# Four convolution layers on one core: the last part of the dense sum on two engines, its statistics partly combined early, the first pair's taps apart, and the loads for the next image in another order

## What is computed

```
# _gn: groups of 2 channels, mean and variance over the group's pixels
x = x + depthwise(_gn(x), kernels from means, w1, b1, w2, b2)   # layer 0
x = x + conv3x3(sign(_gn(x)), sign(W))                          # layer 1, dense over 32 channels
x = x + depthwise(_gn(x), ...)                                  # layer 2
x = x + depthwise(_gn(x), ...)                                  # layer 3
# depthwise: pooled = mean of each channel; hdn = relu(pooled @ w1 + b1);
# kernels = hdn @ w2 + b2, one 3x3 filter for each image and channel
```

## Times and the profile before

| | us |
|---|---|
| median of three runs | 4344.64 |
| lowest and highest | 4337.99, 4358.8 |
| the profiled execution, device time | 4354.15 |
| its span in the trace | 4352.3 |
| TensorE busy | 3142.5 (72% of the span) |
| VectorE, ScalarE, POOL busy | 2069.2, 1786.4, 1957.0 |

### The profile page before, as it was taken

One profiled execution on the slowest core, in us unless ns is written; L12 is line 12 of the kernel. 1 busy time (PEld: TensorE's weight loads), 2 busy tenths in 40 slices (PEclk: granted clock), 3 DMA queues, 4 the chain that ended last, 5 costly groups with the idle time before them and its releaser, 6 DMA issues.

```text
span 4352.3 us, 69714 instructions
## 1 busy us (share of the span) xinstructions
PE 3142.5 (72%) x26176; PEld 2008.6 (46%) x26176; DVE 2069.2 (48%) x6038; ACT 1786.4 (41%) x2626; POOL 1957.0 (45%) x3175
## 2 busy tenths in 40 slices
PE   0675987758876588865887667867778759777598
PEld 0443645435454354633545434554445535445355
DVE  2626643266432764327543275333844257432573
ACT  2433633335333463434534354333543436324232
POOL 1326544264432653336533464425643265431754
PEclk9987998879988798987998879888889889888799
DMA  6288697876969769596694967969678697786946
GB/s 210 57 147 168 151 318 200 155 164 140 340 175 170 159 159 322 159 195 153 182 330 119 212 148 197 306 118 216 149 217 292 109 212 165 234 270 111 200 76 218
DMA packets 589270, 829.46 MB, mean 191 GB/s; under 512 B 489731, under 2 KB 490502, under 8 KB 572550
## 3 DMA queue, kind: packets, MB, share of 16 engines
q1 hardware_dynamic: 323200, 734.28, 66.5%
q10 hardware_dynamic: 216582, 76.68, 8.2%
q0 software_dynamic: 49152, 14.05, 2.0%
HBM read 375.89 MB, written 267.45 MB: 148 GB/s over the span
## 4 chain that ended last, share of the span: by engine, by line
PE 46%; DMA 21%; DVE 9%; SPq 8%; ACT 5%; POOL 4%; ACTq 3%; issue 3%; DVEq 0%; POOLq 0%
PE acc L961 26%; PE acc L978 14%; SPq L327 6%; DMA dense_out<-arena 5%; DMA out<-y 4%; DMA arena<-x 4%; POOL y L510 4%; PE acc L1040 3%; DMA arena<-signs 3%; DVE dense_stats L860 2%; DMA signs<-arena 2%; DMA arena<-y 2%; ACT arena L599 2%; ACTq L535 2%; ACTq L606 2%
## 5 line engine op out<-in xcount | busy, mean ns | idle before, releaser
L961 PE MATMUL acc<-y,arena 64*128 64x384 f32 x9216 | 1749.3, 508 | 190.1 <-ACT y L568 129.0
L961 PEld LDWEIGHTS acc<-y,arena 64*128 64x128 f32 x9216 | 1013.6, 197 | 777.4 <-ACT y L568 229.2
L327 POOL DMA_DIRECT2D arena<-y x1536 | 790.6, 522 | 837.3 <-PE acc L978 736.4
L568 ACT ACTIVATE y<-acc 128x768 f32<-128x768 f32 x832 | 645.1, 807 | 1177.5 <-PE acc L978 1176.6
L978 PE MATMUL acc<-arena 64*128 64x384 f32 x4608 | 953.9, 509 | 195.2 <-issue 195.2
L489 POOL TENSOR_SCALAR arena<-arena,cst,fill 128x24 f32<-128x24 f32 (+1 forms) x1536 | 614.3, 419 | 701.8 <-issue 450.4
L510 POOL TENSOR_TENSOR y<-arena,y 128x3072 f32<-128x3072 f16 x88 | 529.8, 6043 | 734.5 <-DMA arena<-dense_out 734.3
L860 DVE BATCH_NORM_STATS2 dense_stats<-y 128x6 f32<-128x192 f32 x1536 | 408.0, 345 | 728.4 <-POOL y L510 728.2
L978 PEld LDWEIGHTS acc<-arena 64*128 64x128 f32 x4608 | 518.1, 196 | 422.3 <-issue 228.2
L1040 PE MATMUL acc<-arena,wd_side 128*32 128x384 fp8e4 (+1 forms) x10752 | 470.4, 329 | 290.3 <-DMA arena<-signs 231.5
L802 DVE TENSOR_SCALAR_CACHE_REDUCE y<-acc 128x768 f32<-128x768 f32 x256 | 245.1, 958 | 624.3 <-PE acc L978 624.3
(11 more groups left out here) (84 smaller groups left out, 1145.6 us busy)
## 6 DMA issues: line engine op xcount, KB each, us to landing
y<-x SPq DMA_DIRECT2D x64, 2304.0 KB, 26.1
out<-y SPq DMA_DIRECT2D x64, 2304.0 KB, 23.6
arena<-y SPq DMA_DIRECT2D x768, 141.0 KB
arena<-x SPq DMA_DIRECT2D x168, 576.0 KB, 6.4
dense_out<-arena ACTq DMA_DIRECT2D x384, 192.0 KB, 6.9
arena<-dense_out SPq DMA_DIRECT2D x192, 384.0 KB, 6.8
arena<-y SPq DMA_DIRECT2D x768, 71.9 KB
arena<-signs SPq DMA_DIRECT2D x192, 250.0 KB, 10.4
```

The costliest lines, as they stand in the source:

```text
L327: eng.dma_start(halo[at:at + n, slot, :, d0:d0 + size], y[source:source + (n - 1) * step + 1:step, first + odd:first + odd + 3:2, s0:s0 + ...
L568: nc.scalar.activation(y[:, 2 * g:2 * g + 2, k * KN:(k + 1) * KN], acc[:, 2 * k:2 * k + 2, 0:KN], ACT.Identity, accum_out=sums[:, g, k:k + ...
L961: nc.tensor.matmul(acc[:, 2 * k + odd, 0:KN], w_center[at, slot, 2 * q + odd, :], y[at, 2 * g + odd, k * KN:(k + 1) * KN], start=turn == 0 ...
```

## The change

There are four parts.

1. End of the dense layer. POOL also adds the upper 8 channels of the twelfth half, VectorE only the lower 8 (`D_SHARED`). The statistics of the first five windows are combined into one block ahead of the last addition; at the end three blocks per channel are combined, of unequal size.
2. Start of each depthwise layer. A small product of 18 columns (`ps_first`) gives the taps of the first pair, ahead of the full product of 288. `first_weights` turns pair 0's centre taps and writes its weights, then batch 0's halo weights, then pair 1's centre, then the rest; what was one pass over all halo taps is now two, and the centre taps take three passes where they took two.
3. Places in the accumulator memory. Means and variances of `li` 1 and `li` 2 go to banks 5 and 4, other small tiles change places between banks 6 and 7, and TensorE's wait for `fill_ready` ahead of the group variance falls away in `li` 1 and `li` 2.
4. Loads for the next image. ScalarE takes statistics g - 1 behind the copies of pair g, where it took statistics g; the last, 23, now falls in `li` 2 behind pair 8. In SP's queue loads 0 and 1 move ahead of the second and third halo batch of `li` 1, and the loads from 3 on move behind a later halo batch. POOL clears the staging area one batch later.

```diff
@@ sync
-                for b in range(HALO_SLOTS):
-                    halos(first + b)
+                halos(first)
                 for i in range(AHEAD_SLOTS):
                     load_ahead(s, i)
+                for b in range(1, HALO_SLOTS):
+                    halos(first + b)
                 for b in range(BATCHES):
-                    load_ahead(s, 2 * b + AHEAD_SLOTS)
                     halos(first + b + HALO_SLOTS)
-                    load_ahead(s, 2 * b + AHEAD_SLOTS + 1)
+                    for i in (2 * b + AHEAD_SLOTS - 1, 2 * b + AHEAD_SLOTS):
+                        if i >= AHEAD_SLOTS:
+                            load_ahead(s, i)
...
-                    for i in range(2):
-                        load_ahead(s, PAIRS + AHEAD_SLOTS + 2 * b + i)
+                    for i in (PAIRS + 1 + 2 * b, PAIRS + 2 + 2 * b):
+                        load_ahead(s, i)
@@ gpsimd
-                        for n in range(WINDOWS * D_HALVES - 1):
+                        for n in range(WINDOWS * D_HALVES):
...
+                            first = D_SHARED if n == WINDOWS * D_HALVES - 1 else 0
...
-                        if li == 2 and s < B - 1 and b == AHEAD_LATE // 2 + 1:
+                        if li == 2 and s < B - 1 and b == AHEAD_LATE // 2 + 2:
                             clean_stage(s + 1)
@@ scalar
                     evict(d + 1, g)
-                    if s < B - 1:
-                        ahead_stats(s, g)
+                    if s < B - 1 and g > 0:
+                        ahead_stats(s, g - 1)
...
-                        if g < AHEAD_LATE:
-                            ahead_stats(s, PAIRS + g)
+                        if g <= AHEAD_LATE:
+                            ahead_stats(s, PAIRS + g - 1)
@@ vector
-            def first_centers(d):
-                dve.wait_ge(taps_ready, d + 1)
-                turn_centers(slice(0, BATCH_CH))
-                center_weights(d, 0, BATCH_PAIRS)
+            def first_weights(d):
+
+                dve.wait_ge(first_taps_ready, d + 1)
+                turn_centers(slice(0, 2), ps_first.rearrange("p (c t) -> p c t", t=TAPS))
+                pair_centers(d, 0)
+                dve.wait_ge(taps_ready, d + 1)
+                turn_halos(slice(0, BATCH_PAIRS))
                 halo_weights(0)
-                turn_centers(slice(BATCH_CH, C))
+                turn_centers(slice(2, BATCH_CH), by_tap[:, 2:BATCH_CH])
+                pair_centers(d, 1)
+                turn_centers(slice(BATCH_CH, C), by_tap[:, BATCH_CH:C])
+                turn_halos(slice(BATCH_PAIRS, PAIRS))
...
@@ vector, dense
+                add_blocks((agg[:, :, 0], agg[:, :, 1]), early, [WN // 2] * (2 * (WINDOWS - 1)))
...
-                at = y[:, D_CH:C, w * WN:(w + 1) * WN]
-                nc.vector.tensor_tensor(at, d_in[:, n % D_SLOTS], at, ALU.add).then_inc(d_added_last, 1)
+                at = y[:, D_CH:D_CH + D_SHARED, w * WN:(w + 1) * WN]
+                nc.vector.tensor_tensor(at, d_in[:, n % D_SLOTS, 0:D_SHARED], at, ALU.add).then_inc(d_added_last, 1)
...
+                add_blocks((agg[:, :, 0], agg[:, :, 1]), end, [(WINDOWS - 1) * WN, WN // 2, WN // 2])
@@ tensor
-                pe.wait_ge(fill_ready, d + 1)
-                group_sums(ps_var, spread[:]).then_inc(group_var_ready, 1)
+                if d % ND == 0:
+                    pe.wait_ge(fill_ready, d + 1)
+                group_sums(ps_var[d % ND], spread[:]).then_inc(group_var_ready, 1)
...
+                nc.tensor.matmul(ps_first, hidden[:], w2_sb[:, li, 0:2 * TAPS], start=False, stop=True)\
+                    .then_inc(first_taps_ready, 1)
                 nc.tensor.matmul(ps_taps, hidden[:], w2_sb[:, li, :], start=False, stop=True).then_inc(taps_ready, 1)
```

More of the change, by code:

```diff
@@ L70 @@
 D_CH = C // D_HALVES
+D_SHARED = D_CH // 2
 A_HALO = 0
@@ L861, in window_stats, with add_blocks @@
                 return last
+            def add_blocks(to, blocks, counts):
+                means, spreads = blocks[:, :, :, 1], blocks[:, :, :, 2]
+                n = means.shape[2]
+                whole = sum(counts)
+                mean, spread_of = to
+                if len(set(counts)) == 1:
+                    link(nc.vector.tensor_reduce(mean, means, AX.X, ALU.add))
+                    link(nc.vector.tensor_scalar(mean, mean, 1.0 / n, None, ALU.mult))
+                    link(nc.vector.tensor_tensor(means, means, mean.unsqueeze(2).to_broadcast([P, C, n]), ALU.subtract))
+                    link(nc.vector.scalar_tensor_tensor(means, means, float(counts[0]), means, ALU.mult, ALU.mult))
+                else:
+                    weights = dense_stats[:, :, 0, 0:n]
+                    part = dense_stats[:, :, 1, 0:n]
+                    link(nc.vector.tensor_tensor(part, means, weights, ALU.mult))
+                    link(nc.vector.tensor_reduce(mean, part, AX.X, ALU.add))
+                    link(nc.vector.tensor_scalar(mean, mean, 1.0 / whole, None, ALU.mult))
+                    link(nc.vector.tensor_tensor(means, means, mean.unsqueeze(2).to_broadcast([P, C, n]), ALU.subtract))
+                    link(nc.vector.tensor_tensor(part, means, weights, ALU.mult))
+                    link(nc.vector.tensor_tensor(means, means, part, ALU.mult))
+                link(nc.vector.tensor_tensor(spreads, spreads, means, ALU.add))
+                link(nc.vector.tensor_reduce(spread_of, spreads, AX.X, ALU.add))
             def dense(s):
-                adds = WINDOWS * D_HALVES - 1
+                adds = WINDOWS * D_HALVES
                 for w in range(WINDOWS - 1):
@@ L867, in dense @@
                         dve.wait_ge(d_added, s * adds + w * D_HALVES + half + 1)
-                        window_stats(w, half)
+                        last = window_stats(w, half)
+                link(last)
+                rows = dense_stats[:].rearrange("p c w s -> p c (w s)")
+                early = rows[:, :, 0:6 * (WINDOWS - 1)].rearrange("p c (b k) -> p c b k", k=3)
+                end = rows[:, :, 6 * (WINDOWS - 1) - 3:].rearrange("p c (b k) -> p c b k", k=3)
+                add_blocks((agg[:, :, 0], agg[:, :, 1]), early, [WN // 2] * (2 * (WINDOWS - 1)))
```

127 lines of the change are left out of this document (66 added, 61 removed).

## The result

The changed kernel takes 4552.57 us (median of 4, 4547.59 to 4558.82), the kernel before 4345.62 (median of 4): a ratio of 1.0461, with a 95% interval of 1.0432 to 1.0491. It is slower by 207 us, and the forecast was slower by 162. The profiled execution took 4551.96 us, its span is 4550.1, so 197.8 more than the span before.

The account below looks back on a forecast made before the run. No engine bounds the whole: TensorE, the chain through VectorE and the transfers each bound a stretch. Terms 137 + 21 - 14 + 18 + 0 = +162 us gave 4516, 4507 for the median, range 4435 to 4585.

Follow-up runs that it names:

- e9: Changed kernel with part 4 undone, all dense-layer additions on POOL without early combination, and ScalarE copying pair 0's first third in `li` 2: 4355.21 us, ratio 0.9999.
- e11: e9 with loads 0 and 1 behind the first halo batch of `li` 1 and not behind the third: 4299.43 us, ratio 0.9884.
- e10: Kernel before with two edits: POOL does all dense-layer additions (twelfth half in two pieces), ScalarE copies pair 0's first third in `li` 2: 4346.57 us, ratio 0.9993.

## What to carry to other kernels

Where VectorE and POOL work side by side, compare the end times of a VectorE instruction with those of POOL's, not its length with its usual length: a wait can lie inside the busy time. Work that is put ahead of time hides nothing if it waits for the engine that it is meant to run beside; here it was better to leave the additions to POOL whole and let VectorE do what doesn't wait. In a queue that issues in order, look at what a load stands behind before its consumer is moved, and when a stage is made shorter, at which load now comes too late: e9 lost some 50 us that way, as e11 shows.

## What was not expected of the hardware

A VectorE multiplication of 32 elements a partition took 1.05 to 2.06 us beside a running POOL addition (L891, above), and this in the same kernel when none ran (ns, shortest, median, longest):

```profile
L899 DVE TENSOR_SCALAR agg<-agg x8: 182/184/184, 411.5 to 4322.3; 128x32 f32<-128x32 f32 x8
```

Reductions and statistics beside POOL kept their length (0.61 us for 0.62, 4.25 for 4.19). The wait is nowhere in the list of waits.

A wait of 4.8 us on TensorE costs 1.8 more in the matmuls behind it. At the first wait of `li` 1 twenty of them take 4.93 us, against 3.39, and 4.93 to 6.54 at all 21. The granted clock is at the lower of its two levels there in part of the twenty (0.70 of full speed on average over the 4.93 us). So such a wait in this kernel is to be priced at its length and some 40% more (6.6 / 4.8). That isn't a rate for shorter ones: in the kernel before, waits of 0.73 to 1.83 us at pair 1 of `li` 2 left the twenty at 3.50, those of 2.14 to 2.17 took them to 5.19, and in e10 two waits of 2.89 and 2.94 left them at 3.50.
